# Gated cross attention with an expert layer: batch 0's x loaded, normed and projected in two halves, the masks' loads behind the first

## Chip, cores and metric

One core of one Trainium2 chip. The metric is the device time of the whole kernel in microseconds, the median of several executions.

## What is computed

The inputs are x (2 batches of 512 tokens, 256 wide), a context of 2 x 1024 rows (256 wide), a mask of 2 x 512 x 1024 bytes that is true where a key is hidden, and the weights. In float32:

```python
x = x + tanh(g_xattn) * xattn(layernorm(x), ctx, ctx, mask, Wq, Wk, Wv, Wo, bo)   # 16 heads of 64
x = x + tanh(g_ffn) * ffn(layernorm(x), Wg, bg, W1, b1, W2, b2)                   # 8 experts, each token takes the one of the largest gate

def xattn(q, k, v, mask, ...):
    dots = einsum('bhid,bhjd->bhij', heads(q @ Wq), heads(k @ Wk)) * 64 ** -0.5
    dots = where(mask, -finfo.max, dots)
    return merge(softmax(dots) @ heads(v @ Wv)) @ Wo + bo

def ffn(x, ...):   # per token: expert e = argmax(x @ Wg + bg)
    return gelu(x @ W1[e] + b1[e]) @ W2[e] + b2[e]
```

The mask of these inputs leaves each batch few keys to look at. The kernel looks at the mask first, finds for each batch the blocks of 64 keys that matter to any token, and works on a window of three such blocks (192 keys) if they fit in it, as they do here.

## The kernel before

Each engine runs its own list of instructions in order, written out by hand, and waits on semaphores. There is no planner: the order of calls in each engine's block is the order of the work. Tokens lie on 128 partitions, in tiles of 128: a batch has 4 (QT = 4), both have 8 (TT).

**Loads.** SP (block at L364) issues x of batch 0 (load_x, L366), wq, the mask of batch 0 (load_mask, L370), x and mask of batch 1, wk and wv, all without a wait (L374 to L381). It then waits for visit_ready, reads the window from SBUF and loads the context rows (load_window_ctx, L396), then wo and b2. ACT issues six small loads (L642 to L647).

**The start, batch 0.** DVE (L999) waits for x of batch 0 and calls variance over its 4 tiles (L919: one bn_stats for each tile, a wait for the last, one bn_aggr for each tile, which ends in var_ready). ACT's std1(0) (L652) takes the roots, DVE's norm (L927) takes the reciprocal and writes the 4 normed tiles into xn. PE's xn_transposes(0) (L1419) transposes them, two 128 x 128 blocks for each tile, into banks 4 and 5 of PSUM. ACT copies bank 4 (L670) and DVE bank 5 (L1003) into xnT.

**The q projection.** project_q(b, m) (L1481) makes 128 of the 1024 columns of q for the 512 tokens of a batch: two matmuls (c = 0, 1) over 256 inputs into bank m % 4. In float32 each of them is two records in the trace, so that an m has four. ACT empties the even banks and DVE the odd ones (take_q, L675 and L936). So m = 4 to 7 wait until the m four before has been taken: q_act or q_dve at L1483. PE's loop over m = 0 to 7 (L1749) has visit_sums (L1429) and the two small transposes of b1 behind m = 2.

**The mask.** any_visible(b) (L941) is DVE's: two reductions over the bytes of the mask of a batch, and four small steps. PE's visit_sums adds up their results over the partitions, and DVE's find_windows (L957) makes the windows of it and raises visit_ready. SP, ACT, PE and POOL wait for visit_ready before what lies behind the projection.

**The orders at the start.** DVE: variance(0..3), norm, the copy of bank 5, any_visible(0), any_visible(1), take_q(0, 1), find_windows, the copy of b1T, wait for x of batch 1, variance(4..7), take_q(0, 3), norm(4..7), take_q(0, 5), take_q(0, 7). ACT: std1(0), the copy of bank 4, take_q(0, 0), std1(1), the tanh of the gates (with the load of an activation table), take_q(0, 2), take_q(0, 4), take_q(0, 6). PE: xn_transposes(0), wait for wq, m = 0 to 7; then window_context(0) (L1509: transposes of the context rows), xn_transposes(1), and attend_window (L1519: k at L1588, v at L1571, then scores, transposes and values for each of 16 steps). The rest of the kernel (attention of both batches, output projection, routing, experts) isn't touched.

**Semaphores that the change renumbers.** pro_ps counts the groups of transposes of xn (bank 4 and bank 5 of a batch, one each), pro_act and pro_dve the copies of them, var_ready the calls of variance.

## Time and profile before

| | us |
|---|---|
| median of 3 runs | 241.98 (241.69 to 244.35) |
| the profiled execution | 242.49 |
| its span, first to last instruction | 240.7 |
| PE busy in it | 217.7 (90%) |
| DVE busy | 134.3 (56%) |
| ACT busy | 112.5 (47%) |
| mean granted TensorE clock | 0.989 |

The profile is of one execution, and its times count from the first instruction. In the rows PE is TensorE's matmuls, PEld its weight loads, DVE VectorE, ACT ScalarE, POOL GpSimd and SP SyncE, whose queue issues most loads. A timeline row has the start, how long the group lasted, engine, line, operation, out<-in, shapes and the count, and in brackets how long the engine stood idle before it and what released it. A matmul's duration has its latency in it; how often one starts is read from where the next one starts. Tiles are given by the program's names: `s_bank` is banks 0 to 3, `bank` banks 4 to 7, `rows` holds x, and xn lies in the memory of `pT`.

### The profile page before, as it was taken

What the parts mean: (1) busy time and instruction counts of PE and PEld (TensorE: products, weight loads), DVE (VectorE), ACT (ScalarE), POOL (GpSimd) and SP (SyncE); (2) the same over time, 40 slices, a digit from 0 to 9 for tenths busy, and PEclk for the clock granted to TensorE, in tenths of its full rate; (3) what the DMA queues carried; (4) which work ended last, traced back from release to release, by engine and by line L of the source; (5) the groups of instructions that cost most, each with busy time, mean ns of one, the idle gap of its engine ahead of it and who ended that gap; (6) DMA issues with size and microseconds to landing.
All of it is one profiled execution on the core that took longest, in us unless ns stands there. A gap on an engine that the chain in (4) does not pass through costs nothing.

```text
span 240.7 us, 4102 instructions
## 1 busy us (share of the span) xinstructions
PE 217.7 (90%) x1316; PEld 145.8 (61%) x1316; DVE 134.3 (56%) x537; ACT 112.5 (47%) x386; POOL 90.5 (38%) x96
## 2 busy tenths in 40 slices
PE   0499999999999999999999799999999999959960
PEld 0334394456555544488894356565568899948950
DVE  0797424678878722325227777788883435345520
ACT  2101443877887721301234868778844034525420
POOL 5000710555544591000001657755483000776450
PEclk9999999999999999999999999999999999999995
DMA  3990658999990000091000100240000000235011
GB/s 113 365 394 26 183 234 252 331 317 313 233 316 13 0 3 1 0 297 52 3 1 0 46 3 22 62 143 0 0 3 1 3 0 0 82 112 162 31 49 30
DMA packets 21250, 25.24 MB, mean 105 GB/s; under 512 B 1875, under 2 KB 19805, under 8 KB 21088
## 3 DMA queue, kind: packets, MB, share of 16 engines
q1 hardware_dynamic: 19200, 22.58, 30.4%
q0 software_dynamic: 1152, 2.12, 2.6%
q8 instruction: 14, 0.23, 0.5%
q10 hardware_dynamic: 864, 0.15, 0.3%
q14 instruction: 20, 0.16, 0.2%
HBM read 14.21 MB, written 11.68 MB: 108 GB/s over the span
## 4 chain that ended last, share of the span: by engine, by line
PE 68%; issue 12%; DMA 6%; DVE 5%; POOL 4%; ACT 3%; POOLq 0%; DVEq 0%
PE s_bank L1491 11%; PE s_bank L1531 10%; PE bank L1560 8%; PE bank L1563 7%; PE bank L1450 6%; PE bank L1544 5%; PE s_bank L1588 4%; PE s_bank L1776 3%; PE bank L1545 3%; PE bank L1548 3%; DMA oT<-sorted_rows 2%; PE bank L1571 2%; PE bank L1787 2%; DMA rows<-in_x_dram 2%; POOL sorted_rows L537 2%
## 5 line engine op out<-in xcount | busy, mean ns | idle before, releaser
L563 POOL TENSOR_TENSOR probs<-probs,r_col 128x768 f32<-128x768 f32 x32 | 46.9, 1466 | 86.5 <-DVE r_col L1148 86.5
L717 ACT ACTIVATE probs<-probs,negm_run 128x192 f32<-128x192 f32 x128 | 57.1, 448 | 19.5 <-DVE negm_run L1173 19.5
L1173 DVE CUSTOM_DVE_ANT_0 probs<-s_bank,maskneg 128x192 f32<-128x192 f32 x128 | 39.5, 348 | 8.6 <-PE s_bank L1531 8.6
L1491 PE MATMUL s_bank<-xnT,wq_sb 128*128 128x512 f32 x64 | 31.7, 644 | 1.2 <-ACT xnT L670 0.6
L1182 DVE COPY pT<-bank 128x512 f32<-128x512 f32 x32 | 22.1, 691 | 13.6 <-PE bank L1545 13.6
L1531 PE MATMUL s_bank<-k_sb,q_sb 64*128 64x192 f32 x256 | 29.5, 349 | 0.0
L1450 PE MATMUL bank<-wo_sb,oT 128*128 128x256 f32 x128 | 28.7, 380 | 0.0
L1450 PEld LDWEIGHTS bank<-wo_sb,oT 128*128 128x128 f32 x128 | 23.9, 190 | 3.9 <-issue 0.9
L1531 PEld LDWEIGHTS s_bank<-k_sb,q_sb 64*128 64x128 f32 x256 | 20.0, 186 | 9.0 <-issue 7.9
L717 ACT ACTIVATION_READ_ACCUMULATOR probs<-probs,negm_run 128x1 f32 x128 | 24.1, 188 | 0.0
L1491 PEld LDWEIGHTS s_bank<-xnT,wq_sb 128*128 128x128 f32 x64 | 12.6, 206 | 16.4 <-issue 15.0
L1560 PE MATMUL bank<-pT,v_sb 128*64 128x256 f32 x128 | 20.9, 404 | 0.2 <-ACT pT L727 0.2
L1563 PE MATMUL bank<-pT,v_sb 64*64 64x256 f32 x128 | 20.8, 402 | 0.0
L552 POOL DMA_INDIRECT out_dram<-oT x16 | 15.8, 988 | 9.7 <-DVE oT L1121 7.5
L1544 PE MATMUL bank<-ident,probs 128*128 128x128 f32 x64 | 17.5, 300 | 2.0 <-POOL probs L563 1.2
L727 ACT COPY pT<-bank 128x256 f32<-128x256 f32 x32 | 11.9, 370 | 15.7 <-PE bank L1548 15.4
L537 POOL DMA_INDIRECT sorted_rows<-rows,place x8 | 8.0, 1006 | 25.5 <-DVE place L1065 23.9
L1544 PEld LDWEIGHTS bank<-ident,probs 128*128 128x128 f32 x64 | 8.9, 139 | 14.2 <-issue 11.2
L1776 PE MATMUL s_bank<-k_sb,q_sb 128*128 128x128 f32 x128 | 17.1, 277 | 0.1
L1787 PE MATMUL bank<-oT,k_sb 128*128 128x256 f32 x64 | 16.4, 383 | 0.0
L1776 PEld LDWEIGHTS s_bank<-k_sb,q_sb 128*128 128x128 f32 x128 | 15.7, 192 | 0.5 <-ACT k_sb L808 0.4
L1545 PE MATMUL bank<-ident,probs 128*128 128x128 f32 x64 | 15.7, 273 | 0.0
(141 smaller groups left out, 288.5 us busy)
## 6 DMA issues: line engine op xcount, KB each, us to landing
sorted_rows<-empty_row SPq DMA_DIRECT2D x8, 1040.0 KB, 13.3
oT<-in_L_ffn_W_dram SPq DMA_DIRECT2D x1, 2048.0 KB, 17.6
q_sb<-in_L_ffn_W_dram SPq DMA_DIRECT2D x1, 2048.0 KB, 8.4
oT<-sorted_rows SPq DMA_DIRECT2D x1, 1040.0 KB, 6.6
oT<-sorted_rows SPq DMA_DIRECT2D x8, 130.0 KB, 2.2
rows<-in_x_dram SPq DMA_DIRECT2D x2, 512.0 KB, 7.8
wq_sb<-in_L_xattn_Wq_dram SPq DMA_DIRECT2D x1, 1024.0 KB, 8.3
mask_sb<-in_mask_BxSxS_bk_dram SPq DMA_DIRECT2D x2, 512.0 KB, 9.9
```

Of the source, the lines that this page charges most:

```text
L563: nc.gpsimd.tensor_tensor(part, part, r_col[:, u % PB].rearrange("p i h -> p (i h)") .unsqueeze(2).broadcast_to([P, 4, keys]), ALU.mult).t ...
L717: last = nc.scalar.activation(window_part(u, i, h), window_part(u, i, h), ACT.Exp, bias=negm_run[at], scale=-1.0, accum_out=l_run[at])
L1173: nc.vector.tensor_tensor_reduce(window_part(u, i, h), s_bank[u % 2][:, h, i * CK:i * CK + WK], maskneg[:, q, 0:WK], -SCALE, LARGEST, ALU. ...
L1182: nc.vector.tensor_copy(pT[:, u % 2, 0].rearrange("p t n -> p (t n)"), bank[4]).then_inc(first.pT_dve, 1)
L1450: last = nc.tensor.matmul(bank[6 + tt % 2][:, 0:D], oT[:, b, m, q * P:(q + 1) * P], wo_sb[:, m, :], start=(m == 0), stop=(m == M - 1))
L1491: last = nc.tensor.matmul(bank[m % 4], wq_sb[:, c, m * P:(m + 1) * P], xnT[:, c, b * N:(b + 1) * N], start=(c == 0), stop=(c == DC - 1))
L1531: last = nc.tensor.matmul(s_bank[u % 2][:, h, i * CK:i * CK + WK], q_sb[head_rows[h], b, m, q * P:(q + 1) * P], k_sb[head_rows[h], m, 0:WK ...
L1544: nc.tensor.transpose(bank[4][:, i * P:(i + 1) * P], tiles[:, i, 0], ident[:])
L1545: last = nc.tensor.transpose(bank[4][:, CK + i * P:CK + (i + 1) * P], tiles[:, i, 1], ident[:])
L1560: nc.tensor.matmul(to[head_rows[h], 0:CK], v_sb[:, 0, (h * M + m) * DH:(h * M + m + 1) * DH], pT[:, u % 2, h, 0, :], start=True, stop=False)
L1563: last = nc.tensor.matmul(to[head_rows[h], 0:CK], v_sb[head_rows[h], 1, m * DH:(m + 1) * DH], pT[head_rows[h], u % 2, 0, 1, :], start=Fals ...
L1776: last = nc.tensor.matmul(hT_bank(e)[:, ic * P:(ic + 1) * P], w1_sb[:, e, c, ic * P:(ic + 1) * P], sxT[:, e % 2, c * P:(c + 1) * P], start ...
```

## The change

SP loads x of batch 0 as two halves of 256 tokens, each with a semaphore, then wq, and waits until the first half has landed before it issues the mask of batch 0 and all that stands behind. DVE, ACT and PE norm, take roots of, transpose and copy each half by itself. PE projects m = 0 to 3 of half 0 (half_q(0, m)), with the transposes of tiles 2 and 3 behind m = 1; then m = 0 to 3 of half 1, and m = 4 to 7 whole. visit_sums and the transposes of b1 move from behind m = 2 to behind m = 4. DVE takes take_q(0, 3) ahead of the variance of batch 1.

```diff
--- before.py
+++ after.py
@@ -256,6 +256,7 @@
         bank = [s_bank[0][:, 0], s_bank[0][:, 1], s_bank[1][:, 0], s_bank[1][:, 1]] + [b[:] for b in one_bank]
 
         s_x = [sem(f"s_x{b}") for b in range(B)]
+        s_x_half = sem("s_x_half")
         s_wq = sem("s_wq")
         s_mask = [sem(f"s_mask{b}") for b in range(B)]
         s_wk = sem("s_wk")
@@ -371,8 +372,11 @@
                 sp.dma_start(mask_sb[:, b * QT:(b + 1) * QT, :],
                              mask[b].rearrange("(q p) k -> p q k", p=P)).then_inc(s_mask[b], 16)
 
-            load_x(0)
+            for half, landed in enumerate((s_x_half, s_x[0])):
+                sp.dma_start(x_sb[:, 2 * half:2 * half + 2, :],
+                             x[0, half * 2 * P:(half + 1) * 2 * P].rearrange("(q p) d -> p q d", p=P)).then_inc(landed, 16)
             sp.dma_start(wq_sb[:], wq.rearrange("(c p) n -> p c n", p=P)).then_inc(s_wq, 16)
+            sp.wait_ge(s_x_half, 16)
             load_mask(0)
             for b in range(1, B):
                 load_x(b)
@@ -649,14 +653,15 @@
 
             nc.scalar.activation(warm[:], eps[:], ACT.Sqrt)
 
-            def std1(b):
-                act.wait_ge(var_ready, b + 1)
-                nc.scalar.activation(std[:, b * QT:(b + 1) * QT],
-                                     rows[:, b * QT:(b + 1) * QT, VAR:VAR + 1].rearrange("p t o -> p (t o)"), ACT.Sqrt,
+            def std1(k):
+
+                a, z = ((0, 2), (2, QT), (QT, TT))[k]
+                act.wait_ge(var_ready, k + 1)
+                nc.scalar.activation(std[:, a:z], rows[:, a:z, VAR:VAR + 1].rearrange("p t o -> p (t o)"), ACT.Sqrt,
                                      bias=eps[:]).then_inc(std_ready, 1)
 
             def std2(tt):
-                act.wait_ge(var_ready, B + tt + 1)
+                act.wait_ge(var_ready, B + 1 + tt + 1)
                 nc.scalar.activation(std[:, tt:tt + 1], rows[:, tt, VAR:VAR + 1], ACT.Sqrt,
                                      bias=eps[:]).then_inc(std_ready, 1)
 
@@ -665,9 +670,11 @@
                 nc.scalar.copy(xnT[:, :, tt * P:(tt + 1) * P],
                                xt2_bank(tt).rearrange("p (c n) -> p c n", c=DC)).then_inc(xt2_sb, 1)
 
-            std1(0)
-            act.wait_ge(pro_ps, 1)
-            nc.scalar.copy(xnT[:, 0, 0:N], bank[4]).then_inc(pro_act, 1)
+            for half in range(2):
+                std1(half)
+                at = slice(half * 2 * P, (half + 1) * 2 * P)
+                act.wait_ge(pro_ps, 2 * half + 1)
+                nc.scalar.copy(xnT[:, 0, at], bank[4][:, at]).then_inc(pro_act, 1)
             done = act.alloc_register("act_done")
             act.reg_mov(done, 0)
             left = act.alloc_register("act_left")
@@ -780,7 +787,7 @@
             for m in range(0, M, 2):
                 take_q(0, m)
                 if m == 0:
-                    std1(1)
+                    std1(2)
                     act.wait_ge(s_small, 16 * 5)
                     nc.scalar.activation(gate[:], gate_in[:], ACT.Tanh).then_inc(gate_ready, 1)
             def later_visits(b):
@@ -826,9 +833,9 @@
                     take_ctxT(first, 0)
                 else:
                     take_window_ctxT(0)
-                act.wait_ge(pro_ps, 3)
+                act.wait_ge(pro_ps, 5)
                 nc.scalar.copy(xnT[:, 0, N:T], bank[4]).then_inc(pro_act, 1)
-                act.wait_ge(pro_ps, 4)
+                act.wait_ge(pro_ps, 6)
                 nc.scalar.copy(xnT[:, 1, N:T], bank[5]).then_inc(pro_act, 1)
                 for b in range(B):
                     if b > 0:
@@ -996,11 +1003,20 @@
                 nc.vector.tensor_copy(visit[:, :, 1:NC + 2], visit_no[:]).then_inc(visits_listed, 1)
                 dve.wait_ge(visits_listed, 1)
 
+            def take_xnT(half):
+
+                at = slice(half * 2 * P, (half + 1) * 2 * P)
+                dve.wait_ge(pro_ps, 2 * half + 2)
+                nc.vector.tensor_copy(xnT[:, 1, at], bank[5][:, at]).then_inc(pro_dve, 1)
+
+            dve.wait_ge(s_x_half, 16)
+            variance(range(2))
+            norm(0, 2, xn, ln_ready)
             dve.wait_ge(s_x[0], 16)
-            variance(range(QT))
-            norm(0, QT, xn, ln_ready)
-            dve.wait_ge(pro_ps, 2)
-            nc.vector.tensor_copy(xnT[:, 1, 0:N], bank[5]).then_inc(pro_dve, 1)
+            variance(range(2, QT))
+            take_xnT(0)
+            norm(2, QT, xn, ln_ready)
+            take_xnT(1)
             any_visible(0)
             any_visible(1)
             take_q(0, 1)
@@ -1008,8 +1024,8 @@
             dve.wait_ge(b1_ps, 1)
             nc.vector.tensor_copy(b1T[:].rearrange("p c e -> p (c e)"), bank[7][:, 0:IC * E]).then_inc(b1_ready, 1)
             dve.wait_ge(s_x[1], 16)
+            take_q(0, 3)
             variance(range(QT, TT))
-            take_q(0, 3)
             norm(QT, TT, xn, ln_ready)
             for m in range(5, M, 2):
                 take_q(0, m)
@@ -1416,14 +1432,14 @@
             pe.sem_inc(later.ctxT_ps, 1)
             pe.wait_ge(ident_ready, E + 3)
 
-            def xn_transposes(b):
-
-                for i in range(QT):
+            def xn_transposes(b, tiles=range(QT)):
+
+                for i in tiles:
                     pe.wait_ge(ln_ready, b * QT + i + 1)
                     for c in range(DC):
                         last = nc.tensor.transpose(bank[4 + c][:, i * P:(i + 1) * P],
                                                    xn[:, b * QT + i, c * P:(c + 1) * P], ident[:])
-                        if i == QT - 1:
+                        if i == tiles[-1]:
                             last.then_inc(pro_ps, 1)
 
             def visit_sums():
@@ -1431,9 +1447,24 @@
                 nc.tensor.matmul(bank[6][0:1, 0:B * NB], ones[:, 0:1], visit_p[:].rearrange("p b c -> p (b c)"),
                                  start=True, stop=True).then_inc(visit_ps, 1)
 
-            xn_transposes(0)
+            def half_q(half, m):
+
+                at = slice(half * 2 * P, (half + 1) * 2 * P)
+                for c in range(DC):
+                    if m == 0:
+
+                        pe.wait_ge(pro_dve if c else pro_act, half + 1)
+                    last = nc.tensor.matmul(bank[m % 4][:, at], wq_sb[:, c, m * P:(m + 1) * P], xnT[:, c, at],
+                                            start=(c == 0), stop=(c == DC - 1))
+                if half:
+                    last.then_inc(q_ps, 1)
+
+            xn_transposes(0, range(2))
             pe.wait_ge(s_wq, 16)
-            pe.wait_ge(pro_act, 1)
+            for m in range(4):
+                half_q(0, m)
+                if m == 1:
+                    xn_transposes(0, range(2, QT))
             done = pe.alloc_register("pe_done")
             pe.reg_mov(done, 0)
             left = pe.alloc_register("pe_left")
@@ -1485,9 +1516,6 @@
 
                     pe.wait_ge(first.negm_ready, 4 * (b * PER - 1 + m // 2))
                 for c in range(DC):
-                    if b == 0 and m == 0 and c == 1:
-
-                        pe.wait_ge(pro_dve, 1)
                     last = nc.tensor.matmul(bank[m % 4], wq_sb[:, c, m * P:(m + 1) * P],
                                             xnT[:, c, b * N:(b + 1) * N], start=(c == 0), stop=(c == DC - 1))
                 last.then_inc(q_ps, 1)
@@ -1591,7 +1619,7 @@
                     last.then_inc(first.k_ps, 1)
                     also(f"k{u}")
                 pe.wait_ge(s_wv, 16)
-                pe.wait_ge(pro_act, 3)
+                pe.wait_ge(pro_act, 4)
                 pe.wait_ge(b1_ready, 1)
                 if b > 0:
                     pe.wait_ge(x2_ready, b * QT)
@@ -1686,7 +1714,7 @@
                     last.then_inc(S.k_ps, 1)
                     also(f"k{u}")
                 pe.wait_ge(s_wv, 16)
-                pe.wait_ge(pro_act, 3)
+                pe.wait_ge(pro_act, 4)
                 pe.wait_ge(b1_ready, 1)
                 if b > 0:
                     pe.wait_ge(x2_ready, b * QT)
@@ -1747,8 +1775,11 @@
                 pe.wait_ge(first.pT_dve, (b + 1) * PER)
 
             for m in range(M):
-                project_q(0, m)
-                if m == 2:
+                if m < 4:
+                    half_q(1, m)
+                else:
+                    project_q(0, m)
+                if m == 4:
                     visit_sums()
                     pe.wait_ge(s_b1, 16)
                     for ic in range(IC):
```

## Rows read from the trace of the kernel before

**Rows 1.** Page, part 4: the chain that ended last, by engine

```profile
PE 68%; issue 12%; DMA 6%; DVE 5%; POOL 4%; ACT 3%; POOLq 0%; DVEq 0%
```

**Rows 2.** The chain in order of time, 0 to 50 us: start, us, what

```profile
0.78 5.12 DMA rows<-in_x_dram
...
11.47 8.06 PE s_bank L1491 x12
...
21.66 1.32 DVE stats L921 x4
...
23.73 1.28 ACT L785
...
25.76 3.70 PE s_bank L1491 x8
```

**Rows 3.** Timeline of PE, 8 to 32 and 97 to 119: start, us

```profile
8.89 1.94 PE L1424 MATMUL bank<-ident,pT 128*128 128x128 f32 x8 [8.89 <-DVE pT L933]
...
19.82 5.42 PE L1491 MATMUL s_bank<-xnT,wq_sb 128*128 128x512 f32 x12
...
101.29 7.07 PE L1450 MATMUL bank<-wo_sb,oT 128*128 128x256 f32 x32
```

**Rows 4.** DMA issues, 0 to 50 us: count, KB each, median us to landing

```profile
wq_sb<-in_L_xattn_Wq_dram SPq DMA_DIRECT2D x1, 1024.0 KB, 8.3
mask_sb<-in_mask_BxSxS_bk_dram SPq DMA_DIRECT2D x2, 512.0 KB, 9.9
...
ctx_sb<-in_ctx_dram SPq DMA_DIRECT2D x2, 128.0 KB, 2.1
```

**Rows 5.** Timeline of DVE, 5 to 31 us

```profile
5.93 1.41 DVE L921 BATCH_NORM_STATS2 stats<-rows 128x6 f32<-128x256 f32 x4 [5.82 <-DMA rows<-in_x_dram]
...
8.33 1.39 DVE L933 TENSOR_SCALAR pT<-rows 128x256 f32<-128x256 f32 x4
10.86 0.69 DVE L1003 COPY xnT<-bank 128x512 f32<-128x512 f32 x1 [1.15 <-PE bank L1424]
11.47 2.33 DVE L947 TENSOR_REDUCE rowmin<-mask_sb 128x32 f32<-128x1024 uint16 x2
...
17.99 0.18 DVE L954 TENSOR_TENSOR visit_p<-fullb,blockmin 128x16 f32<-128x16 f32 x1
18.08 0.68 DVE L939 COPY q_sb<-s_bank 128x512 f32<-128x512 f32 x1
19.79 0.18 DVE L961 TENSOR_SCALAR block_seen<-bank 1x32 f32<-1x32 f32 x1 [1.03 <-PE bank L1431]
...
23.30 0.66 DVE L939 COPY q_sb<-s_bank 128x512 f32<-128x512 f32 x1
23.87 0.17 DVE L931 RECIPROCAL rows<-std 128x4 f32<-128x4 f32 x1
```

**Rows 6.** Timeline of SP, which issues the loads

```profile
1.28 0.50 SPq L375 DMA_DIRECT2D wq_sb<-in_L_xattn_Wq_dram  x1
1.83 0.46 SPq L371 DMA_DIRECT2D mask_sb<-in_mask_BxSxS_bk_dram  x1
```

**Rows 7.** q matmuls in stretches: us, PE, PEld busy (count), clock, DMA, GB/s

```profile
12.30:16.70 4.40, 4.40 (x6) 1.69 (x5) 1.00 1.06 398
```

**Rows 8.** Timeline of the weight loads (PEld), 11 to 19 us

```profile
12.46 0.34 PEld L1491 LDWEIGHTS s_bank<-xnT,wq_sb 128*128 128x128 f32 x1 [0.52 <-issue]
13.31 0.34 PEld L1491 LDWEIGHTS s_bank<-xnT,wq_sb 128*128 128x128 f32 x1 [0.52 <-issue]
```

**Rows 9.** Timeline of ACT, 3 to 32 us

```profile
25.14 1.05 ACT L677 COPY q_sb<-s_bank 128x512 f32<-128x512 f32 x2
```

**Rows 10.** Timeline of PE near the end, 210 to 241 us

```profile
215.47 0.77 PE L1765 MATMUL s_bank<-ident,xnT 128*128 128x128 f32 x4 [2.29 <-DVE xnT L1106]
...
230.54 2.01 PE L1787 MATMUL bank<-oT,k_sb 128*128 128x256 f32 x8
```

**Rows 11.** Stretches at the end: busy of five engines, clock, DMA, GB/s

```profile
234.00:236.00 2.00, 0.00 (x0) 0.00 (x0) 0.00 (x0) 0.00 (x0) 0.98 (x1) 0.83 0.41 90
```

## The prediction, made before the change was timed

> **What bounds the kernel now.** I read the chain of work that ended last first. By engine it is mostly TensorE [rows 1]: the kernel is paced by the PE queue, so a stall of PE before the attention starts moves the end one for one unless something later has slack. The same chain over the first 50 us [rows 2] shows the stretch that the change rewrites. The reader is to see three things there. The load of x holds everything to 5.9 us. PE then projects q from 11.47 us. And the chain leaves PE at 19.5 us, goes through DVE (find_windows, then the statistics of batch 1 at 21.66) and ACT (a table load at 23.73) and comes back to PE at 25.76, which is m = 6 of the q projection. That detour exists because m = 6 needs bank 2, bank 2 is emptied by ACT's take_q(0, 2), and that stands in ACT's queue behind std1(1) and the tanh, hence behind DVE's variance(4..7), hence behind find_windows. At present the detour costs little: PE waits only 0.5 us for it, as the twelve matmuls from 19.82, which last 5.42 us, cover it [rows 3].
>
> **Part 1, x in two halves.** The whole x of batch 0 lands 5.12 us after its issue [rows 2]; 128 KB land 2.1 us after issue [rows 4]. x of batch 0 is 512 KB, and a half (256 KB) is estimated between: about 1 us earlier, at 4.9 us. DVE's statistics take 1.41 us for four tiles and the norm 1.39 us [rows 5], so two tiles save another 1.3 us before the last xn of the first step is there. The first half's four transposes are half of eight in 1.94 us [rows 3]. So xnT of half 0 is there at about 8.7 us. But the first q matmul also needs wq, issued at 1.28 and landed 8.3 us later, at 9.6 [rows 4, 6]. wq now ends the wait. Taken: PE starts q at 9.8 instead of 11.47, 1.7 us earlier. Bounds: 8.7, from where the norm is the later of the two, if taking the masks out from behind wq frees the engines for it (the 1.25 MB of x and wq behind the first half take 3.1 us at the 398 GB/s of [rows 7], which would land wq at 8.1), 10.5 if the extra issue (0.5 us) and a gap add up.
>
> **Part 2, masks held back.** SP now waits until about 4.9 us before it issues mask 0 (1.83 before, [rows 6]); x of batch 1, mask 1, wk and wv are queued behind. wq is still being moved then (it lands at 9.6), so the engines should not run dry: cost nothing to 0.5 us on each later landing. The two masks took 9.9 us from issue in the median, with all that stood before them [rows 4]; with less ahead of it mask 0 lands near 11.5; by the next part DVE reads it only at 14.6. That cover goes only if it lands more than 3 us late.
>
> **Part 3, PE's new order.** PE does m = 0 and 1 on half 0 (8 matmuls of 256 columns), then the transposes of tiles 2 and 3, then m = 2 and 3 on half 0, then half 1. The columns are the same; a 256 column matmul costs 7.07/32 = 0.22 us at the full clock, half of the 0.44 us between 512 column ones (the twelve from 19.82: 5.42 less the 0.6 of the last, over 11) [rows 3], so halving costs nothing in itself. But the clock: matmuls of 512 columns start every 0.85 us at first (their weight loads at 12.46 and 13.31, [rows 8]). The granted clock reads 1.00 there [rows 7], but the spacing is that of the lower level (1.2 GHz against 2.4). The twelve from 11.47 last 8.06 us [rows 2], which with the two spacings makes about 5.5 us at the lower level. So the first 8 half matmuls cost 8 x 0.427 = 3.4 us: 9.8 to 13.2. The four transposes behind them take 1.94 - 4 x 0.22 = 1.1 us: tiles 2 and 3, normed by about 9.7, are transposed only at 14.3.
>
> **Part 4, DVE's order, which decides.** take_xnT(1) waits for those transposes, and DVE is in order: both any_visible, take_q(0, 1), find_windows and the variance of batch 1 are behind it. At present the mask reduction starts at 11.47, right after the one xnT copy of 0.69 us [rows 5]. Now: transposes end 14.3, a copy of half the size 0.35, so the reduction starts at 14.65, 3.2 us later. The two any_visible last from 11.47 to 18.17, 6.7 us [rows 5]: 21.35. take_q(0, 1) takes 0.6: 21.95. Before, DVE sat idle 1.03 us at that point for PE's visit sum (find_windows at 19.79, [rows 5]). Now PE has m = 4 done at about 21.7 (9.8 + 5.5 us low, with 10 of the 32 half matmuls and the transposes in it, 22 more at 0.216 us, m = 4 in 1.7 us) and the sum by 22.0, so that idle microsecond absorbs part: find_windows starts at about 22.0, +2.2 us. Then take_q(0, 3) stands before the variance instead of behind it: from 23.30 to 23.87, +0.57 us [rows 5]. All that follows (std1, table load, tanh, take_q(0, 2) and the next from 25.14, [rows 9]) moves by 2.2 + 0.57 = 2.8 us. PE starts m = 6 at 25.76 + 2.8 = 28.5. The 1.7 us that PE gained are spent: it runs m = 5 when take_q(0, 1) has emptied bank 1 (22.1 to 23.8), and then stands idle 4.7 us.
>
> Bounds of this part: with q started at 8.7 and the full clock at once the transposes would end at 11.0 (1.7 us of matmuls, 0.55 of transposes), and m = 6 would start at about 25.2, 0.6 us early; with q started at 10.5 and a clock that rises late it would be 31, over 5 us late. I take 2.8, as the two rows nearest to it (5.5 us low, wq 8.3 us after issue) give it.
>
> **Part 5, the clock after the hole.** No idle stretch of 4.7 us lies between matmuls before. The nearest rows are at the end: PE's last matmuls run from 230.54 for 2.01 us, to 232.55, and the mean granted clock of 234 to 236 is 0.83 [rows 10, 11], so the last (1 - 0.83) x 2 / 0.5 = 0.7 us were at the lower level: it fell at 235.3, 2.8 us after the last matmul. A gap of 2.29 us (to 215.47) did not end in slow matmuls [rows 10]: the four transposes behind it took 0.77 us, where eight took 1.94 at the lower level [rows 3]. 4.7 us is clearly on the side where it falls. Price: m = 6, 7 and the k projection then run at the lower level. How long is taken from the start: 5.5 us from the first q matmul, half of which is loss: 2.7 us. Bounds: 0 (it holds), and 4.0 if it stays low as long as from the first transposes at 8.89 to 17 us. PE paces the stretch behind m = 6, so this adds in full.
>
> Nothing behind gives it back: context, k and the scores follow on PE, and ctx lands long before (2.1 us after an issue that follows find_windows). Sum: 2.8 + 2.7 = +5.5 us. On the profiled execution: 242.49 + 5.5 = 248.0; its time is 0.5 above the median of the runs, which I take as the base: 241.98 + 5.5 = 247.5.
>
> **The rivals.** (a) The clock holds over the hole (or the hole is nearer 3 us). For it: the fall came in one place only and may not repeat. Against: 2.8 us were enough there. Time: 241.98 + 2.8 = 244.8. (b) Not slower: wq lands before 8.5 because the masks are out of its way, and the clock rises within the first matmuls; DVE's chain is then on time and the hole is the old 0.5 us. It decides at the end of the second transposes: if that lies before 11.5 us, nothing is late, and 241.4 to 242.5 follows (some 0.6 gained). For it: SP's masks really did share the queue with wq. Against: in [rows 2, 8] the lower level lasted 5.5 us of matmuls, and x, issued first, was on DVE's hands at 5.93 with wq and the masks queued behind it, so what stands behind a load in this queue seems not to hold it up. (c) The first rise of the clock is late, since transposes now interrupt the matmuls. If the 5.5 us are counted only from 14.3, the lower level lasts to 19.8: 21 half matmuls done by then, 11 x 0.216 + 1.7 = 4.1 more to the end of m = 4, 23.9. The visit sum is then PE's again: find_windows at 24.2, +4.4, m = 6 at +5.0; with the fall behind it +7.7: 249.7. For it: before, with transposes from 8.89, the clock did not rise before 16.9. Against: they stood alone then, ahead of the matmuls and with a gap behind them, and the clock rose all the same. The Trainium skill (TensorE: Matmul & The Clock Gate, Part 4: PE-mode transpose) says that the full clock does not engage for transposes, which it does not count as TensorE being busy. The trace agrees so far as the transposes of [rows 3] were followed by slow matmuls. (d) The change does what its words say, but the gain is hidden: PE's start moves and m = 6 does not, which is (b) without its 0.6.
>
> **How the numbers follow.** Forecast (late DVE and fallen clock) 0.55, its own range 246.3 to 248.9; (a) 0.20; (c) 0.08; (b) and (d) 0.15; the rest 0.02. The range goes from 244.0, which takes in (a) and leaves out (b), to 249.8, which takes in (c) and the 4.0 of the clock. 1% (2.4 us) is about what a measurement of this kernel can tell from no change. Slower by over 1% means over 244.4: the forecast, (c) and most of (a), 0.80. Within 1%: (b), (d) and the low end of (a), 0.17. Faster by over 1% has no mechanism that the bounds reach: 0.03.
>
> **What would show it.** In the profile after: the first bn_stats near 5.0 us; the first q matmul at 9.6 to 10 (8.6 would speak for b); the second group of transposes at 13 to 14.3; DVE's mask reduction at 14.6, not 11.5; find_windows at 22; ACT's table load before the tanh at 26.4; PE idle some 4.7 us before m = 6 and matmuls every 0.85 us behind it. The prediction is wrong in its size if the spacing behind the hole is 0.43 us, and wrong in its sign if the mask reduction starts before 12 us.

## The result, and the profile after

| | before | changed |
|---|---|---|
| median of the runs, us | 242.28 (4 runs, 241.69 to 244.35) | 250.5 (4 runs, 248.27 to 251.82) |
| ratio | 1 | 1.031 (1.0262 to 1.0357) |
| profiled execution, us | 242.49 | 248.27 |
| its span | 240.7 | 246.7 |
| mean granted clock | 0.989 | 0.970 |

The change makes the kernel 3.1% slower. The forecast was slower by 5.5 us: 248.0 for the profiled execution, which took 248.27, and 247.5 for the median, which is 250.5. Ratios compare the fast runs of the kernels alone, since some executions of one and the same kernel take a per cent or two more.

The chain of the changed kernel over the first 46 us, in order of time (start, us, what), answers to [rows 2]:

```profile
1.80 7.66 DMA wq_sb<-in_L_xattn_Wq_dram
...
9.50 3.78 PE s_bank L1457 x8
13.29 0.53 PE bank L1440 x4
13.84 0.42 DVE xnT L1010
14.26 2.26 DVE rowmin L954 x2
...
17.57 2.27 DVE rowmin L954 x2
...
20.87 0.34 DVE q_sb L946
...
21.39 0.18 DVE block_seen L968
...
23.16 0.68 DVE q_sb L946
23.84 1.32 DVE stats L928 x4
...
25.91 1.28 ACT L792
...
27.94 6.59 PE s_bank L1519 x8
```

What the reader is to see: in [rows 2] the chain stayed on PE from 11.47 to 19.5 us and made a short detour over DVE. Now it begins with wq instead of x, leaves PE at 13.8 with the copy of xnT (L1010) and stays on DVE and ACT until m = 6 at 27.94: both mask reductions (L954), take_q(0, 1) at 20.87, find_windows (L968) at 21.39, take_q(0, 3) at 23.16, the variance, the table load. PE is no longer what bounds this stretch.

The same on PE (timeline: start, us, engine, line, form, count, and in brackets the idle time before and its releaser), and the first scores of the attention, a mark that is used below:

```profile
9.50 3.78 PE L1457 MATMUL s_bank<-xnT,wq_sb 128*128 128x256 f32 x8 [1.46 <-DMA wq_sb<-in_L_xattn_Wq_dram]
...
20.92 0.22 PE L1447 MATMUL bank<-visit_p,ones 128*1 128x32 f32 x2 [0.23 <-DVE visit_p L961]
...
21.52 1.98 PE L1519 MATMUL s_bank<-xnT,wq_sb 128*128 128x512 f32 x4 [0.16 <-DVE q_sb L946]
27.94 6.59 PE L1519 MATMUL s_bank<-xnT,wq_sb 128*128 128x512 f32 x8 [4.43 <-ACT q_sb L684]
...
43.17 0.92 PE L1559 MATMUL s_bank<-k_sb,q_sb 64*128 64x192 f32 x8
```

PE starts q at 9.50 instead of 11.47, and m = 6 at 27.94 instead of 25.76, after 4.43 us in which it has nothing. And the eight matmuls of m = 6 and 7 last 6.59 us, where they lasted 3.70 [rows 2]. The stretches show why (us, its length, busy time and count of PE, PEld, DVE, ACT and POOL, granted clock, DMA share, GB/s):

```profile
24.00:26.00 2.00, 0.00 (x0) 0.00 (x0) 1.60 (x9) 0.39 (x2) 0.00 (x0) 1.00 0.13 31
26.00:28.00 2.00, 0.06 (x1) 0.07 (x1) 1.96 (x6) 1.99 (x4) 0.29 (x1) 0.74 0.38 110
28.00:30.00 2.00, 2.00 (x3) 0.97 (x4) 0.12 (x1) 0.37 (x1) 1.92 (x2) 0.50 0.59 164
...
32.00:34.00 2.00, 2.00 (x4) 0.73 (x3) 0.00 (x0) 0.34 (x1) 1.23 (x1) 0.55 1.07 406
34.00:36.00 2.00, 2.00 (x13) 1.26 (x12) 0.69 (x1) 0.48 (x1) 0.00 (x0) 1.00 0.55 229
```

The granted clock is at 1.00 (2.4 GHz) until 26 us, goes to 0.50 (1.2 GHz) near 27 us, inside the hole, and is back at 1.00 from 34 us. The lower level lasts some 6.8 us, through m = 6 and 7.

In the kernel before, the first scores start at 38.10 us (same view):

```profile
38.10 0.92 PE L1531 MATMUL s_bank<-k_sb,q_sb 64*128 64x192 f32 x8
```

So the change costs 5.07 us by that mark, and two numbers make it up: m = 6 starts 2.18 us later, and from m = 6 to the scores it is 15.23 us instead of 12.34, which is 2.89 us for the clock. All of it is still there 170 us later. The last eight matmuls of the experts' first layer (L1776, in the changed kernel L1807) ahead of the gap near the end of the kernel are a second mark; they start at

```profile
210.28 1.05 PE L1776 MATMUL s_bank<-k_sb,q_sb 128*128 128x128 f32 x8
```

in the kernel before and 5.07 us later in the changed one:

```profile
215.35 1.05 PE L1807 MATMUL s_bank<-k_sb,q_sb 128*128 128x128 f32 x8
```

The span grew by 6.0, so 0.9 us more are lost behind this mark. PE's last matmuls start 5.92 us later (236.46 against the 230.54 of [rows 10]). In between the clock is low once more, behind a gap of 1.93 us on PE (218.25 to 220.17); by these stretches it fell at about 221.5, when PE had been at work again for over 1 us:

```profile
220.00:222.00 2.00, 1.68 (x10) 1.33 (x11) 1.08 (x4) 0.69 (x2) 1.39 (x3) 0.88 0.61 180
222.00:224.00 2.00, 2.00 (x11) 2.00 (x11) 1.09 (x4) 0.89 (x3) 1.64 (x2) 0.50 0.59 168
224.00:226.00 2.00, 2.00 (x12) 1.85 (x11) 0.05 (x1) 0.62 (x2) 0.98 (x1) 0.76 0.53 148
```

The same gap is 2.29 us long in [rows 10], and the clock stayed up.

### The profile page after: what moved, and what is told of

Read it like the earlier page. It is cut to its first block, busy times and chain, and to the rows that moved or that the text cites. A ratio compares the mean times of both kernels' runs of the same rounds, so it can differ in the third digit from the quotient of the medians.

```text
span 246.7 us, 4140 instructions
## 1 busy us (share of the span) xinstructions
PE 221.0 (90%) x1332; PEld 151.5 (61%) x1332; DVE 135.1 (55%) x539; ACT 112.7 (46%) x388; POOL 90.5 (37%) x96
## 4 chain that ended last, share of the span: by engine, by line
PE 66%; issue 12%; DVE 7%; DMA 5%; POOL 4%; ACT 3%; SPq 0%; POOLq 0%; DVEq 0%
PE s_bank L1559 9%; PE s_bank L1519 8%; PE bank L1588 7%; PE bank L1591 7%; PE bank L1481 6%; PE bank L1572 5%; PE s_bank L1616 4%; PE s_bank L1807 4%; DMA wq_sb<-in_L_xattn_Wq_dram 3%; PE bank L1573 3%; PE bank L1576 3%; PE bank L1818 2%; PE bank L1599 2%; DVE rowmin L954 2%; POOL sorted_rows L541 2%
## 5 line engine op out<-in xcount | busy, mean ns | idle before, releaser
L1519 PE MATMUL s_bank<-xnT,wq_sb 128*128 128x512 f32 x48 | 25.0, 665 | 4.6 <-ACT q_sb L684 4.4
L1519 PEld LDWEIGHTS s_bank<-xnT,wq_sb 128*128 128x128 f32 x48 | 9.7, 214 | 15.7 <-issue 10.2
L1807 PE MATMUL s_bank<-k_sb,q_sb 128*128 128x128 f32 x128 | 18.5, 292 | 0.1
L1807 PEld LDWEIGHTS s_bank<-k_sb,q_sb 128*128 128x128 f32 x128 | 17.0, 205 | 0.5 <-ACT k_sb L815 0.4
```

What stands on the lines that cost most here:

```text
L1519: last = nc.tensor.matmul(bank[m % 4], wq_sb[:, c, m * P:(m + 1) * P], xnT[:, c, b * N:(b + 1) * N], start=(c == 0), stop=(c == DC - 1))
L1807: last = nc.tensor.matmul(hT_bank(e)[:, ic * P:(ic + 1) * P], w1_sb[:, e, c, ic * P:(ic + 1) * P], sxT[:, e % 2, c * P:(c + 1) * P], start ...
```

## The experiments

They ran in three groups, each on one chip (the first and the third on the same), with the kernel before timed beside them: a1, a2, a3 and a4 in the first, a0, a5, b1 and c1_all in the second, a6, b0 and c1_all_again in the third. There the kernel before took 248.85, 251.38 and 248.66 us (medians), not 242. The last group has a profile of it (b0_before_again, below): its early part is the same to 0.1 us, the rest is a stall near the end. So ratios are compared within a group, and the kernels by three marks of the profile that hardly move from chip to chip: the start of m = 6, the first scores behind it, and the matmuls of L1776 ahead of the gap near the end (L1806 to L1810 in the changed kernels).

| kernel | m = 6 starts | hole before it | m = 6 to scores | scores | mark near the end | ratio (95%) |
|---|---|---|---|---|---|---|
| before | 25.76 | 0.52 | 12.34 | 38.10 | 210.28 | 1 |
| b0_before_again | 25.85 | 0.52 | 12.35 | 38.20 | 210.38 | 1.0003 (0.9967 to 1.0039) |
| changed | 27.94 | 4.43 | 15.23 | 43.17 | 215.35 | 1.031 (1.0262 to 1.0357) |
| a0_after_again | 27.69 | 4.43 | 15.22 | 42.91 | 215.10 | 1.0205 (1.0147 to 1.0263) |
| a1_no_sp_wait | 28.54 | 4.54 | 14.05 | 42.59 | 214.76 | 1.0217 (1.0138 to 1.0295) |
| a3_fill | 28.55 | filled | 12.35 | 40.90 | 213.08 | 1.0104 (1.0032 to 1.0175) |
| a5_early_T | 26.95 | 4.53 | 15.42 | 42.37 | 214.56 | 1.0113 (1.006 to 1.0166) |
| a6_sum_first | 27.70 | 2.35 | 14.04 | 41.74 | 213.91 | 1.0209 (1.0148 to 1.0269) |
| a4_early_windows | 24.50 | 2.23 | 12.35 | 36.85 | 209.03 | 1.0026 (0.9988 to 1.0065) |
| a2_act_order | no hole | none | | 36.60 | 208.78 | 0.9969 (0.9925 to 1.0014) |
| b1_before_act_order | no hole | none | | 37.16 | 209.34 | 0.9966 (0.9938 to 0.9994) |
| c1_all | no hole | none | | 34.94 | 207.12 | 0.9949 (0.9903 to 0.9994) |
| c1_all_again | no hole | none | | 34.63 | 206.81 | 0.9932 (0.9889 to 0.9974) |

From the scores to the mark near the end it is 172.17 to 172.19 us in all 13 profiles: nothing between them gives time back or takes more. What differs behind that mark is the gap or stall near the end, and it differs between profiles of kernels that are the same there (see the last group).

### The changed kernel once more

> The changed kernel itself once more, to stand beside the others on one chip and to show whether the holes and the clock repeat. My theory: m = 6 at 27.9 to 28.6 us after a hole of 4.4 us or so, the clock falls in it or just behind it, the first scores at 42.5 to 43.5 us, and a ratio to the kernel before of 1.02 to 1.035. Rival (the loss of the first measurement was of that chip alone): ratio within 1% of 1.

```profile
27.69 6.58 PE L1519 MATMUL s_bank<-xnT,wq_sb 128*128 128x512 f32 x8 [4.43 <-ACT q_sb L684]
...
42.91 0.92 PE L1559 MATMUL s_bank<-k_sb,q_sb 64*128 64x192 f32 x8
```

Hole, fallen clock and scores repeat to 0.3 us, and the ratio says slower here too. 2.05% of 251.38 is 5.2 us, close to the 4.8 us that the early part loses. The 3.1% of the first measurement are 7.5 us, 2.4 more than its early part explains.

### The masks' loads not held back

```diff
-            sp.wait_ge(s_x_half, 16)
             load_mask(0)
```

> The changed kernel with SP's wait for the first half taken out, so that the masks and all loads behind them are issued at once. My theory (the time goes at m = 6, which waits for DVE and ACT, and at the clock behind that hole): the masks land before 14.18 us in both, so nothing moves, m = 6 at about 27.9 us and 248 to 252 us as in the changed kernel. Rival (the held back loads cost the time): the mask reduction starts earlier and the time falls towards 242 to 245.

```profile
9.50 3.78 PE L1456 MATMUL s_bank<-xnT,wq_sb 128*128 128x256 f32 x8 [1.45 <-DMA wq_sb<-in_L_xattn_Wq_dram]
...
28.54 5.40 PE L1518 MATMUL s_bank<-xnT,wq_sb 128*128 128x512 f32 x8 [4.54 <-ACT q_sb L683]
...
42.59 0.92 PE L1558 MATMUL s_bank<-k_sb,q_sb 64*128 64x192 f32 x8
```

q starts at 9.50, as with the wait: what is queued behind wq doesn't hold it up, and the wait gains nothing. Nor does it cost anything: hole and loss stay. m = 6 comes 0.6 us later, as the clock rose later in this execution (the four transposes last 1.06 us instead of 0.72, the 24 half matmuls behind them 6.08 us instead of 5.35). That isn't the edit's doing: a3_fill, which has SP's wait, has its m = 6 at 28.55. And the clock behind the hole costs 1.7 us instead of 2.9. It fell later here, at about 29.0 by these stretches, 0.5 us behind the start of m = 6, and stayed low for 3.4 us instead of 6.8:

```profile
28.00:30.00 2.00, 1.46 (x3) 0.69 (x4) 0.73 (x2) 0.98 (x3) 1.60 (x2) 0.76 0.54 109
...
32.00:34.00 2.00, 2.00 (x6) 0.55 (x4) 0.02 (x1) 0.48 (x1) 1.84 (x1) 0.88 1.12 409
```

### ACT's order alone

```diff
             for m in range(0, M, 2):
                 take_q(0, m)
-                if m == 0:
+                if m == 4:
                     std1(2)
                     ...
```

> The changed kernel with ACT's order alone changed: std1 of batch 1 and the tanh stand behind take_q(0, 4) instead of take_q(0, 0). My theory: m = 6 then has its bank at once, PE goes from m = 5 (21.5 us) through m = 7 to 26.8, waits some 0.7 us for the context rows, the clock stays up, and k starts at about 29.2 us against 31.1 in the kernel before: 240 to 241 us. Rival (the half matmuls, the extra instructions or the loads cost the time): still 247 or more, since none of that is changed.

```profile
21.66 5.42 PE L1519 MATMUL s_bank<-xnT,wq_sb 128*128 128x512 f32 x12 [0.17 <-DVE q_sb L946]
27.73 0.33 PE L1542 MATMUL s_bank<-ident,ctx_sb 128*128 128x128 f32 x1 [0.65 <-DMA ctx_sb<-in_ctx_dram]
...
36.60 0.92 PE L1559 MATMUL s_bank<-k_sb,q_sb 64*128 64x192 f32 x8
```

This is the test that tells most. Nothing of the halves, of PE's order, of the loads or of DVE's order is changed; only take_q(0, 2) no longer stands behind the square root and the table load. The twelve matmuls of m = 5, 6 and 7 run through in 5.42 us, the clock stays up, PE waits 0.65 us for the context rows, and the scores come at 36.60: 6.3 us earlier than in a0_after_again and 1.5 us earlier than in the kernel before. The loss of the change went through that one entry of ACT's queue. The 1.5 us are whole at the mark near the end (208.78). The ratio (0.9969, 0.9925 to 1.0014) can't tell them from nothing; expected were 240 to 241 us where the kernel before takes 242.

### The hole filled with matmuls

```diff
+                    if m == 6:
+                        for _ in range(5):
+                            nc.tensor.matmul(bank[4], wq_sb[:, 0, 0:P], xnT[:, 0, 0:N], start=True, stop=True)
                     project_q(0, m)
```

> The changed kernel with five more matmuls of 512 columns (10 records, about 4.3 us, into the idle bank 4, results not used) ahead of m = 6: PE has work in the hole, and the hole stays as long as it is. My theory of the clock: m = 6 still starts at about 27.9 us, but its matmuls are 0.43 us apart, k starts 2.9 us earlier than in the changed kernel, and the time is 3 to 4 us below it: 245 to 247. Rival (slow matmuls behind the hole have another cause, such as the loads of wo and b2 or POOL's long add beside them): spacing stays 0.85 us, 248 to 252.

```profile
28.55 3.70 PE L1519 MATMUL s_bank<-xnT,wq_sb 128*128 128x512 f32 x8 [0.25 <-ACT q_sb L684]
...
40.90 0.92 PE L1559 MATMUL s_bank<-k_sb,q_sb 64*128 64x192 f32 x8
```

```profile
30.00:32.00 2.00, 2.00 (x6) 0.85 (x5) 0.00 (x0) 0.59 (x1) 2.00 (x1) 1.00 0.89 265
```

m = 6 is as late as ever (28.55), yet the eight matmuls of m = 6 and 7 last 3.70 us, and to the scores it is 12.35 us, as in the kernel before. POOL's addition and the loads still run beside them (POOL busy for the whole of this stretch, DMA at 0.89), and the clock is at 1.00. That isolates the clock: idle PE, and not the loads or POOL's addition, made the matmuls slow. The five matmuls give nothing that is used and still save 1.7 us by the scores against a1_no_sp_wait, whose m = 6 starts at the same time. The ratio is 1.1% lower; the two intervals overlap, but each of the four runs here (251.16 to 252.02 us) is below each of the four there (253.26 to 254.98).

### DVE's chain freed, ACT's order left

```diff
             xn_transposes(0, range(2))
+            xn_transposes(0, range(2, QT))
             pe.wait_ge(s_wq, 16)
             for m in range(4):
                 half_q(0, m)
-                if m == 1:
-                    xn_transposes(0, range(2, QT))
...
-                if m == 4:
+                if m == 3:
                     visit_sums()
...
-            take_q(0, 3)
             variance(range(QT, TT))
+            take_q(0, 3)
```

> The changed kernel with DVE's chain freed: PE transposes tiles 2 and 3 before the first q matmul, visit_sums and the transposes of b1 stand behind m = 3 instead of m = 4, and take_q(0, 3) stands behind the variance of batch 1 again. ACT's order is as in the changed kernel. My theory: the mask reduction starts at about 11.2 us, find_windows is PE's at about 19.3, m = 6 at about 25.3 after a hole of some 2.5 us in which the clock mostly holds: 241.5 to 243, near the kernel before. Rival (the halves themselves cost): 245 or more.

```profile
10.97 2.34 DVE L954 TENSOR_REDUCE rowmin<-mask_sb 128x32 f32<-128x1024 uint16 x2 [0.29 <-DMA mask_sb<-in_mask_BxSxS_bk_dram]
...
18.54 0.18 DVE L968 TENSOR_SCALAR block_seen<-bank 1x32 f32<-1x32 f32 x1 [0.26 <-PE bank L1447]
```

```profile
24.50 3.70 PE L1518 MATMUL s_bank<-xnT,wq_sb 128*128 128x512 f32 x8 [2.23 <-ACT q_sb L684]
...
36.85 0.92 PE L1558 MATMUL s_bank<-k_sb,q_sb 64*128 64x192 f32 x8
```

The mask reduction starts at 10.97 (it now waits 0.29 us for the mask), find_windows at 18.54, m = 6 at 24.50, and the hole of 2.23 us leaves the clock up. The scores come 1.25 us earlier than before, and so does the mark near the end (209.03). The ratio is 1.0026, and its interval leaves out 0.995: the gain is lost behind that mark.

### One of the two locks alone

PE's transposes early, as above, and nothing else:

> The changed kernel with one thing undone: the transposes of tiles 2 and 3 ahead of the first q matmul. visit_sums stay behind m = 4. My theory of two locks: the mask reduction starts at about 11 us, but find_windows then waits for PE's visit sum behind m = 4 and starts at about 20.3, only 1 us earlier than in the changed kernel; m = 6 at 26.9 after a hole of about 4.9 us; ratio 1.01 to 1.03, most of the loss still there. Rival (my prediction's words: take_xnT(1) behind PE's half matmuls is what decides): the loss is gone, ratio 1.005 or less.

```profile
10.98 2.35 DVE L954 TENSOR_REDUCE rowmin<-mask_sb 128x32 f32<-128x1024 uint16 x2 [0.28 <-DMA mask_sb<-in_mask_BxSxS_bk_dram]
...
20.40 0.18 DVE L968 TENSOR_SCALAR block_seen<-bank 1x32 f32<-1x32 f32 x1 [2.12 <-PE bank L1447]
```

```profile
26.95 6.77 PE L1518 MATMUL s_bank<-xnT,wq_sb 128*128 128x512 f32 x8 [4.53 <-ACT q_sb L684]
...
42.37 0.92 PE L1558 MATMUL s_bank<-k_sb,q_sb 64*128 64x192 f32 x8
```

The mask is looked at 3.2 us earlier than in the changed kernel, and find_windows only 1.0 us earlier, since it now waits for PE's visit sum behind m = 4. m = 6 moves by 1 us, the hole is as long, the clock falls all the same.

And the other: visit_sums behind m = 3, take_q(0, 3) behind the variance, transposes left where the change has them:

> The changed kernel with visit_sums and the transposes of b1 behind m = 3 instead of m = 4, and take_q(0, 3) behind the variance of batch 1 again; PE's transposes of tiles 2 and 3 and ACT's order stay as in the changed kernel. DVE's chain stays late. My theory: PE now waits for the masks' result ahead of m = 4 (from 19.0 to 20.9 us), runs m = 4 and 5 to 24.7, and m = 6 starts at 27.3, 0.6 earlier than in the changed kernel. The hole before it is only 2.6 us, so the clock holds, and the first scores come 12.3 us behind m = 6 as in the kernel before, at 39.7: ratio 1.003 to 1.015, half of the loss gone, though m = 6 hardly moved. Rival (the clock falls whenever m = 6 is late): scores at 42 or later, ratio 1.02.

```profile
21.28 0.22 PE L1447 MATMUL bank<-visit_p,ones 128*1 128x32 f32 x2 [1.78 <-DVE visit_p L961]
...
27.70 5.40 PE L1519 MATMUL s_bank<-xnT,wq_sb 128*128 128x512 f32 x8 [2.35 <-ACT q_sb L684]
...
41.74 0.92 PE L1559 MATMUL s_bank<-k_sb,q_sb 64*128 64x192 f32 x8
```

Here my expectation failed. The idle time is split, as expected, into 1.78 us before the visit sum and 2.35 us before m = 6, but the clock fell, at about 28.0, 0.3 us behind the start of m = 6: 14.04 us to the scores, 1.7 lost. So a hole of 2.35 us, with the 1.78 us some 4 us of work before it, cost the clock here; 2.23 and 2.29 us (a4_early_windows, [rows 10]) did not, and 1.93 us near the end of the changed kernel did. The length of the hole alone doesn't tell. Whether the earlier 1.78 us had a part in it isn't shown.

### ACT's order in the kernel before, and everything together

> The kernel before (x in one load) with only ACT's order changed: std1 of batch 1 and the tanh behind take_q(0, 4). My theory: only its small hole of 0.5 us before m = 6 goes, ratio 0.996 to 1.0, first scores near 37.7. Rival (ACT's order is worth as much without the halves): 1% or more faster.

> The changed kernel with all locks taken away together: transposes of tiles 2 and 3 ahead of the first q matmul, visit_sums behind m = 3, take_q(0, 3) behind the variance of batch 1, and ACT's std1 and tanh behind take_q(0, 4). My theory: q from 10.0 us with no hole to m = 7 at about 25.4, first scores at 34.5 to 35 against 38.2 in the kernel before: 3.3 us faster, ratio 0.985 to 0.99. Rival (the early part is given back at a later stage): the early part as said and the ratio still 0.995 or more.

> The kernel with all locks taken away, once more. Its first scores came 3.2 us earlier than in the kernel before, and its ratio was 0.9949 (0.9903 to 0.9994). Theory: the early gain is passed on and the rest is the scatter of the late clock, so ratio 0.985 to 0.997. Rival (it is given back late): ratio over 0.997.

The first of them is the kernel before with the edit of a2_act_order, the other two are the changed kernel with the edits of a4_early_windows and a2_act_order. The first scores of b1_before_act_order and of c1_all:

```profile
37.16 0.92 PE L1531 MATMUL s_bank<-k_sb,q_sb 64*128 64x192 f32 x8
```

```profile
34.94 0.92 PE L1558 MATMUL s_bank<-k_sb,q_sb 64*128 64x192 f32 x8
```

ACT's order alone gives the kernel before 0.9 us by that mark (more than the 0.5 us of its hole). The halves with all locks off give 3.2 to 3.5 us; so loading and projecting in halves, in a fitting order, is worth 2.2 to 2.5 us beside ACT's order. As a time c1_all is faster than the kernel before by 0.5% and 0.7%, the intervals just clear of 1, and both figures are less than half of the early gain. The 0.9949 of c1_all stands between its theory (0.985 to 0.99) and its rival (0.995 or more, given back later), and c1_all_again kept its expectation. These are the lowest ratios of the study, but their intervals overlap those of a2_act_order and b1_before_act_order, so that they are faster than these isn't shown. The early gain is whole at the mark near the end (207.12 and 206.81), so what is given back is given back behind it: all kernels of these groups stall there (next), and the clock is low behind the stall for a time that differs from run to run.

### The kernel before in the last group

> The kernel before itself, for a profile of it on a chip on which it takes some 249 to 251 us instead of 242. Theory: the early part is as in the first profile (first scores at 38.1), the ratio is 1, and the 7 to 9 us more lie in a stall of all engines near 210 us with a lower clock behind it. Rival: the early part is longer too, so that the early parts of different chips can't be set side by side.

The stretches near the end (columns as above):

```profile
212.00:215.00 3.00, 0.58 (x3) 0.18 (x1) 0.48 (x1) 0.00 (x0) 2.39 (x3) 1.00 0.59 149
215.00:218.00 3.00, 2.08 (x4) 1.18 (x4) 0.48 (x1) 0.63 (x2) 2.03 (x3) 0.51 0.45 131
218.00:221.00 3.00, 0.00 (x0) 0.00 (x0) 0.21 (x1) 0.00 (x0) 0.98 (x1) 0.50 0.66 203
```

Its scores come at 38.20, as in the first profile. From 212 to 221 us PE is busy for 2.7 us, DVE for 1.2 and ACT for 0.6, and the clock goes to 0.50; in the first profile PE's whole gap there is 2.29 us. The chain of that stretch puts three waits, of 3.03, 4.41 and 2.95 us, to nothing that the core itself ran, as this one:

```profile
212.76 4.41 another core or an unknown queue
```

The stall is in all profiles of these groups, with the change and without. From the mark near the end to the first transposes behind the stall it is 5.19 us in the first profile of the kernel before and 4.82 in that of the changed one, 9.9 to 11.3 in the profiles of the first and third groups and 12.0 to 12.8 in those of the second. These figures don't follow the edits: c1_all has 12.07 and c1_all_again, the same program on the other chip, 10.01, and on one chip the figures differ by up to 1.4 us among themselves. So the end of one profile can't show a gain of 1 or 2 us, and what makes the stall stays open.

## Why the prediction was right, point by point

**Direction and mechanism: right.** Slower, through the two things that were named: m = 6 late behind DVE and ACT, and the clock in the hole that this makes. a2_act_order shows the first (take the entry out of ACT's queue and the loss is gone), a3_fill the second (give PE something to do and the matmuls are fast again). How near the number of the profiled execution came (248.0 said, 248.27 measured) is in part luck: it is the fastest of the four, and a loss that the sum didn't have made up for terms that were too large.

**Part 1, the start: right.** x's half was on DVE at 4.80 us (4.9 said), wq ended the wait, q started at 9.50 (9.8 said). The lower bound, a wq that lands early because the masks are out of its way, is excluded: with and without SP's wait q starts at 9.50.

**Part 2, the held masks: right.** No cost, and no gain either (a1_no_sp_wait).

**Part 3, PE: mis-sized by half a microsecond in the profiled execution.** The low clock was taken for 5.5 us of q matmuls, and it was over after 3.8 in this execution: the four transposes behind the first eight matmuls last 0.72 us and not 1.1, and the mask reduction starts at 14.18 instead of 14.65. The term varies from execution to execution: with the same order the transposes took 0.69 us in a0_after_again and 1.05 to 1.06, as said, in a1, a2, a3 and a6. Rival (c), a rise so late that the lower level lasts to 19.8 us, happened in none of them. The Trainium skill (TensorE: Matmul & The Clock Gate, Part 4: PE-mode transpose) says that transposes don't count as TensorE being busy. These rows can't show it or contradict it, since the eight matmuls came before them.

**Part 4, m = 6: mis-sized, 2.8 said, 2.18 measured.** Mostly the half microsecond of part 3: in a1_no_sp_wait and a3_fill, where the clock rose later, find_windows came at 21.98 and 22.00 and m = 6 at 28.54 and 28.55, against 22.0 and 28.5 said. In the profiled execution take_q(0, 3) cost its 0.6 us (23.16 to 23.75), and find_windows came at 21.39 instead of 22.0. The hole was 4.43 us against 4.7. The text said that DVE's order decides, by the transposes. That was half of it: a5_early_T shows that visit_sums behind m = 4 is a second lock that holds nearly as well, and undoing the transposes alone brings m = 6 only 1 us forward.

**Part 5, the clock: right in kind, 2.7 said, 2.89 measured** (2.87 in a0_after_again, 3.08 in a5_early_T, 1.7 in a1_no_sp_wait). The text had the k projection at the lower level too; its 32 matmuls last 5.37 us, as before, and only m = 6 and 7 are slow. That the lower level lasts as long as it did at the start had no row behind it but that one; by a1_no_sp_wait the price can be 1.7 us as well.

**The sum.** 2.8 + 2.7 = 5.5 was said and 2.18 + 2.89 = 5.07 came, by the first scores; the profiled execution took 5.8 us more than that of before. The sum by the first scores is whole at the mark near the end (5.07 us there too). The 0.9 us that it lacked lie behind that, where the clock falls a second time. The prediction said that nothing behind gives time back, and didn't ask whether something behind takes more. The median is the part that the sum doesn't explain. At 250.5 us it is 3.0 above the 247.5 said and above the 249.8 to which the range goes; only as a ratio is it inside (1.031, where 249.8 to 241.98 is 1.032). It moved by 8.2 us, 2.2 more than the span of the profiled execution: two of the four runs have 250.2 us of span at a mean clock of 0.964, against 246.7 at 0.970. That is (0.036 x 250.2 - 0.030 x 246.7) / 0.5 = 3.2 us more at the lower level, which by an estimate (half of it is loss where PE is busy) costs some 1.6 of their 3.5 us; where they lie, and what the rest is, stays open, as only one execution is profiled.

**Rivals.** (a), the clock holds, was given 0.20, and no profiled execution with a hole over 4 us held it to the end of m = 7. (b), not slower, failed on both of its conditions together. Its sign, that nothing is late if the second transposes end before 11.5 us, doesn't hold either: in a5_early_T they end at 10.2 and the mask reduction starts at 10.98, and the kernel is still 1.1% slower, by the second lock. c1_all shows that its idea was sound once all locks are off.

## What to carry to other kernels

Before a first step is split to start an engine sooner, list what hangs on its second half in each in-order queue: here PE started 2 us earlier and was 2 us late at m = 6, because a side computation (the mask) had lost its place and a copy that PE needed stood behind it in ACT's queue. Moving that copy ahead of the unrelated wait turned the loss into a gain of 1.5 us by the first scores. Price a hole on TensorE twice, once for how late it makes the matmuls behind it (2.18 us here) and once for how slow they are (2.89 us).

## What was not expected

Matmuls whose results nobody reads made the kernel faster than idleness: 12.35 us from m = 6 to the scores with the hole filled, 14.05 to 15.42 with a hole of over 4 us. The Trainium skill (TensorE: Matmul & The Clock Gate, Why this matters for your kernels) warns of long idle gaps between bursts of matmuls and says that one of them brings the lower clock back. The trace agrees for the holes of over 4 us; the falls behind 2.35 and 1.93 us lie below the gap length that it gives, and there the measurement decides.

For holes of about 2 us the outcome varied: 2.23 and 2.29 us kept the clock, 2.35 and 1.93 us lost it, each when PE was already at work again.

The same program, with the same first 38 us, took 242 us in the first measurement and 248 to 251 in the later groups, and its two profiles differ by a stall of three engines near the end.
